# An inverse square root moved from GpSimd to VectorE in the layer norms that run inside four attention layers

## The chip, the cores and the metric

The kernel is one program on one core of a Trainium2 chip. The metric is the device time of that program in microseconds (us), from its first to its last instruction and what lies around them. The engines are named as the profile names them: PE is TensorE (matrix products, transposes), PEld its weight loads, DVE is VectorE, ACT is ScalarE, POOL is GpSimd, SP the engine that issues most DMAs.

## The reference, cut to what matters

Sixteen sequences of 112 tokens with 256 features go through four layers. Each layer is a cross attention against a context of 375 rows, then a feed-forward part, both on the normalised residual stream:

```python
def _layernorm(x, axis=-1, eps=1e-05):
    m = jnp.mean(x, axis=axis, keepdims=True)
    v = jnp.var(x, axis=axis, keepdims=True)
    return (x - m) / jnp.sqrt(v + eps)
...
x = x + _L0_xattn_ref(_layernorm(x), ctx_1024, ...)     # 16 heads of 16
x = x + _L0_ffn_ref(_layernorm(x), ...)                 # 8 experts, 1 chosen, one shared
x = x + _L1_xattn_ref(_layernorm(x), ctx_1024, ...)     # 1 head of 256
x = x + _L1_ffn_ref(_layernorm(x), ...)                 # 8 experts, 2 chosen, two shared
x = x + _L2_xattn_ref(_layernorm(x), ctx_1024, ...)     # 16 heads of 64
x = x + _L2_ffn_ref(_layernorm(x), ...)                 # 8 experts, 2 chosen
x = x + _L3_xattn_ref(_layernorm(x), ctx_1024, ...)     # 16 heads of 16
x = x + _L3_ffn_ref(_layernorm(x), ...)                 # expert 0 alone, then its own layer norm
```

The change touches the four norms ahead of the feed-forward parts: they are computed inside the attention, as soon as a pair of sequences has its new residual. Everything is 32-bit floating point.

## The kernel before

The kernel works layer after layer (L0 to L3), and each layer in three stages with a meeting of PE, DVE and ACT between them: a norm and transposes ahead of the attention, the attention, the feed-forward part. The attention goes over 16 sequences (called b) and in L0, L2 and L3 over 16 heads of each; one head is a **slot** here, numbered 0 to 15 within its sequence. L1 has one head, so one slot is a whole sequence.

The order of work in the attention is one list of steps, `Att.plan`, which PE, DVE and ACT each walk from front to back, doing their own share of each step. In every slot stand the scores of one head (PE line 895 or 900 or 903, the maximum on DVE line 1149, 1160 or 1153), the exponential of a head (ACT line 1196), the transposes of its probabilities (PE 914, copied by DVE 1169 or ACT 1203) and, in L0 and L3, every fourth slot the product with the values for four heads (PE 945). Between them the steps of `extras` are laid: the projections of the next sequence (`gen q`, `gen k`, `gen v`: PE 813, 833, 837; DVE 1060 or 1063, 1072), the split of q and k for an exact product (DVE 1033, 1035), and the steps that finish a sequence: `norm` (DVE 1130, 1133), `gen i` (PE 843), `gen o` (PE 857, DVE 1080 or 1077) and `stats` (DVE 1095).

After the `stats` of every odd sequence come the steps of the norm of that pair of sequences, `("ln", pair, i)` for i from 0 to `LN_STEPS`. With `LN_STEPS` of 4 these are: two `bn_aggr` (line 1107), variance plus epsilon into `newton` (1109), `nmr` = minus mean times `rstd` (1112), and `xn`, two instructions (1120). `rstd`, the inverse square root, is made by POOL between the third and the fourth (line 1299, power of minus one half). Then `gen n` has PE transpose `xn` (864), ACT copies it out (1239), and in L0 to L2 `gen r` multiplies by the router's weights (PE 871, DVE 1087 or 1089). POOL also stores `xn` to memory (1306) in L0 to L2, and in L3 adds a bias (1324).

`follow` places these steps: each one slot after the one before, `gen r` two slots after `gen n`. In L1 all steps of a pair's norm stand in one slot, and in every layer the steps of the last pair stand behind the last slot, where no other work is left. Every step of a norm waits on the semaphore `ln_dve` for the step before it.

Of the kernel before, what the change touches and what calls it, by code (L numbers as in the profile page):

```python
# [26 lines left out]
I32 = mybir.dt.int32  # L27
U8 = mybir.dt.uint8
U32 = mybir.dt.uint32
ALU = mybir.AluOpType  # L30
# [4 lines left out]
B = 16  # L35
S = 112
# [7 lines left out]
CHUNK = 4  # L44
NCH = B // CHUNK
TOK = CHUNK * S
EPS = 1e-5
# [59 lines left out]
LN_STEPS = 4  # L107
# [341 lines left out]
def build(nc, A):  # L449
    ctx = ExitStack()  # L450
    with ctx:
        sb = lambda name, shape, dt=F32: ctx.enter_context(nc.sbuf_tensor(name, shape, dt))
        sem = lambda name: ctx.enter_context(nc.semaphore(name))
# [24 lines left out]
        root = sb("root", [S, CHUNK])  # L478
# [53 lines left out]
        newton = sb("newton", [S, 2])  # L532
# [51 lines left out]
        ln = Ln(sem)  # L584
        fin = sem("final_chain")
        b2_added = sem("b2_added")
        rooted = sem("roots_by_pool")
# [369 lines left out]
        def att_vector(dve, t):  # L957
# [139 lines left out]
            def row_norm(pair, i):  # L1097

                at = ln.at(2 * L + 1)
                two = slice(2 * pair, 2 * pair + 2)  # L1100
                u, y = newton[:, :], rstd[:, two]
                before = [("stats", 2 * pair), ("stats", 2 * pair + 1)] + \
                     [("ln", pair, j) for j in range(1, LN_STEPS)]
                dve.wait_ge(ln.dve, at + t.row_steps[before[i]])
                if i < 2:
                    b = 2 * pair + i
                    ins = dve.bn_aggr(mv[:, b, :], stats[:, b, :])
                elif i == 2:
                    ins = dve.tensor_scalar(u, mv[:, two, 1], EPS, None, ALU.add)  # L1109
                elif i == 3:  # L1110
                    dve.wait_ge(rooted, L * (B // 2) + pair + 1)
                    ins = dve.scalar_tensor_tensor(out=nmr[:, two], in0=mv[:, two, 0], scalar=-1.0, in1=y,
                                                   op0=ALU.mult, op1=ALU.mult)
                else:
                    if t.moe and pair >= 2:
                        f = ffn[L]
                        dve.wait_ge(f.x_stored[pair % 2], f.x_stored0 + 16 * (pair // 2))
                        dve.wait_ge(t.gen_ready, t.g0 + t.gen_index("n", 2 * pair - 3) + 1)
                    for b in (2 * pair, 2 * pair + 1):
                        ins = dve.tensor_scalar(xnr(t, b), xb(b), rstd[:, b:b + 1], nmr[:, b:b + 1], ALU.mult, ALU.add)  # L1120
                    ins.then_inc(ln.xn, 1)
                    return
                ins.then_inc(ln.dve, 1)
# [170 lines left out]
        def reciprocal_root(pool, t, pair):  # L1294

            at = ln.at(2 * t.L + 1)
            two = slice(2 * pair, 2 * pair + 2)
            pool.wait_ge(ln.dve, at + t.row_steps[("ln", pair, 2)])
            pool.tensor_tensor(rstd[:, two], newton[:, :], root[:, 0:2], ALU.pow).then_inc(rooted, 1)  # L1299

        def store_tokens(pool, t, f):

            for pair in range(B // 2):
                reciprocal_root(pool, t, pair)
                pool.wait_ge(ln.xn, (2 * t.L + 1) * (B // 2) + pair + 1)
                pool.dma_start(xnd[f.L][pair * 2 * S:(pair + 1) * 2 * S, :].rearrange("(b s) d -> s b d", s=S),
                               xn[:, pair % 2, :, :]).then_inc(f.x_stored[pair % 2], 16)
# [9 lines left out]
        def add_b2(pool, t, f):  # L1317

            pool.wait_ge(f.w_landed, 16)
            for pair in range(B // 2):  # L1320
                reciprocal_root(pool, t, pair)
# [701 lines left out]
        def _(pool):  # L2023
# [8 lines left out]
            nc.gpsimd.memset(root[:, :], -0.5).then_inc(consts, 1)  # L2032
# [3 lines left out]
            pool.wait_ge(consts, 10)  # L2036
# [12 lines left out]
            pool.wait_ge(consts, 18)  # L2049
# [14 lines left out]
        def _(pe):  # L2064
            pe.wait_ge(consts, 19)
# [9 lines left out]
        def _(act):  # L2075
            act.wait_ge(consts, 19)
# [10 lines left out]
        def _(dve):  # L2087
            dve.wait_ge(consts, 19)
            dve.tensor_reduce(sel2[:, :], sel16[:, :].rearrange("p (j e) -> p e j", e=2), AX_X, ALU.add)\
                .then_inc(consts, 1)  # L2090
            dve.wait_ge(consts, 20)
# [112 lines left out]
```

## Time and profile before

| | us |
|---|---|
| median of 3 runs | 2652.26 (2651.37 to 2652.56) |
| the profiled execution | 2652.56, of it the span from first to last instruction 2650.8 |
| PE busy | 2301.7 (87% of the span) |
| DVE busy | 1263.3 (48%) |
| ACT busy | 1050.3 (40%) |
| POOL busy | 253.3 (10%) |

Busy shares are averages over the whole program. The attention of L0 lies at about 30 to 410 us, that of L1 at 800 to 890, of L2 at 1200 to 1902, of L3 at 2150 to 2500; what a change is worth has to be read in those stretches. Times in the rows further below are microseconds from the start of the span, and a row of the timeline names start, duration, engine, line, operation, output and inputs, and in square brackets how long the engine sat idle before and on what it waited.

### The profile page before, as it was taken

To read this page: it belongs to the slowest core of one execution; us is meant where nothing else is said; L and a number is where in the kernel's file an instruction comes from. 1 tells how busy PE (TensorE), PEld (TensorE's weight loads), DVE (VectorE), ACT (ScalarE), POOL (GpSimd) and SP (SyncE) were. 2 spreads that over 40 slices of the span, in tenths; PEclk is the share of its full clock that TensorE was granted. 3 is DMA by queue.
4 is the path that set the end of the run, shared out by engine and by line. 5 is a ranking of instruction groups with operands and counts; after the bars stand their busy time and mean duration, and the time that the engine had idled before them with its cause. 6 is when DMAs were issued, how large, how long until landed. Compare 5 with 4: busy or idle time off the path is not lost.

```text
span 2650.8 us, 45875 instructions
## 1 busy us (share of the span) xinstructions
PE 2301.7 (87%) x15952; PEld 1782.7 (67%) x15952; DVE 1263.3 (48%) x3635; ACT 1050.3 (40%) x2819; POOL 253.3 (10%) x288
## 2 busy tenths in 40 slices
PE   4889886999969599859999999999689579989893
PEld 3777774777757467547777778777467457777662
DVE  5777773222234522264444444444622457777405
ACT  2777771222113122124444444444212157777510
POOL 0000000111101044100000000000034200000000
PEclk8999996999969699969999999999889879999996
DMA  6877765222244212310000000000322378777200
GB/s 189 194 190 193 190 146 225 80 80 96 62 137 161 109 56 64 80 50 7 16 7 17 11 16 7 11 16 1 122 92 64 87 201 192 191 187 189 69 0 28
DMA packets 149806, 254.19 MB, mean 96 GB/s; under 512 B 14784, under 2 KB 124688, under 8 KB 146912
## 3 DMA queue, kind: packets, MB, share of 16 engines
q1 hardware_dynamic: 138640, 221.09, 30.8%
q0 software_dynamic: 10944, 30.16, 3.6%
q8 instruction: 136, 2.23, 0.4%
q14 instruction: 86, 0.70, 0.1%
HBM read 192.22 MB, written 58.98 MB: 95 GB/s over the span
## 4 chain that ended last, share of the span: by engine, by line
PE 72%; DVE 14%; issue 6%; ACT 4%; DMA 2%; PEld 1%; SPq 0%; POOL 0%; DVEq 0%; PEldq 0%; ACTq 0%; POOLq 0%
PE bank L1619 8%; PE bank L945 6%; PE bank L914 6%; PE bank L1649 6%; PE bank L822 5%; PE bank L826 5%; PE bank L1674 5%; PE bank L900 4%; PE bank L857 4%; PE bank L1662 3%; PE bank L813 3%; DVE arena L1149 3%; PE bank L837 2%; PE bank L1922 2%; PE bank L1908 2%
## 5 line engine op out<-in xcount | busy, mean ns | idle before, releaser
L914 PE MATMUL bank<-ident,arena 112*125 112x112 f32 x2352 | 369.7, 275 | 1.4 <-ACT arena L1203 1.2
L914 PEld LDWEIGHTS bank<-ident,arena 112*125 112x125 f32 x2352 | 340.5, 188 | 39.9 <-issue 2.6
L1196 ACT ACTIVATE arena<-arena,mx 112x375 f32<-112x375 f32 x512 | 309.3, 605 | 140.2 <-DVE mx L1149 136.1
L1149 DVE CUSTOM_DVE_ANT_0 arena<-bank,maskf 112x375 f32<-112x375 f32 x512 | 274.2, 542 | 91.9 <-PE bank L895 75.0
L895 PE MATMUL bank<-kS,qS 128*112 128x376 f32 x512 | 237.6, 465 | 31.5 <-DMA kS<-key_halves 21.2
L945 PE MATMUL bank<-arena 125*32 125x112 f32 (+1 forms) x4608 | 202.0, 264 | 57.7 <-DVE arena L1169 28.9
L1160 DVE TENSOR_REDUCE mx<-bank 112x1 f32<-112x375 f32 x256 | 129.0, 544 | 245.8 <-PE bank L900 245.3
L945 PEld LDWEIGHTS bank<-arena 125*32 125x32 f32 (+1 forms) x4608 | 147.4, 118 | 145.4 <-issue 67.9
L1619 PE MATMUL bank<-arena 128*128 x552 | 238.6, 555 | 3.4 <-ACT arena L1721 3.2
L1169 DVE COPY arena<-bank 125x336 f32<-125x336 f32 x448 | 214.5, 503 | 33.4 <-PE bank L914 33.4
L1196 ACT ACTIVATE arena<-bank,mx 112x375 f32<-112x375 f32 x272 | 156.0, 575 | 172.6 <-DVE mx L1160 150.0
L1203 ACT ACTIVATE arena<-bank 125x336 f32<-125x336 f32 x336 | 147.8, 441 | 72.6 <-PE bank L914 71.8
L1649 PE MATMUL bank<-arena 128*128 (+1 forms) x696 | 173.0, 380 | 0.0
L1299 POOL TENSOR_TENSOR rstd<-newton,root 112x2 f32<-112x2 f32 x32 | 22.6, 707 | 1538.3 <-DVE newton L1109 1538.3
L822 PE MATMUL bank<-ctx_halves,weight_halves 128*128 128x376 f32 x768 | 145.8, 342 | 7.3 <-DVE arena L1066 7.3
L1619 PEld LDWEIGHTS bank<-arena 128*128 128x128 f32 x552 | 103.5, 191 | 68.1 <-issue 48.8
L826 PE MATMUL bank<-weight_halves,ctx_halves 128*126 128x512 f32 x576 | 148.5, 403 | 0.0
L1674 PE MATMUL bank<-xnT,arena 128*128 128x224 f32 (+1 forms) x640 | 143.4, 369 | 3.4 <-DVE gather_id L1446 3.4
L1751 ACT ACTIVATE oT<-bank 128x224 f32<-128x224 f32 x80 | 28.5, 356 | 279.0 <-PE bank L1674 273.5
L822 PEld LDWEIGHTS bank<-ctx_halves,weight_halves 128*128 128x128 f32 x768 | 132.4, 191 | 7.5 <-DVE arena L1066 7.5
L1542 POOL DMA_INDIRECT results<-arena,scatter_id x94 | 93.2, 992 | 411.7 <-ACT arena L1743 332.4
L1674 PEld LDWEIGHTS bank<-xnT,arena 128*128 128x128 f32 (+1 forms) x640 | 111.1, 180 | 30.8 <-issue 16.2
(233 smaller groups left out, 3564.8 us busy)
## 6 DMA issues: line engine op xcount, KB each, us to landing
kS<-key_halves SPq DMA_DIRECT2D x256, 188.0 KB, 5.4
qS<-query_halves SPq DMA_DIRECT2D x128, 224.0 KB, 4.6
arena<-in_ctxT SPq DMA_DIRECT2D x64, 376.0 KB, 4.7
key_halves<-arena SPq DMA_DIRECT2D x64, 376.0 KB, 4.9
arena<-in_f_out SPq DMA_DIRECT2D x22, 768.0 KB, 4.4
query_halves<-arena SPq DMA_DIRECT2D x32, 448.0 KB, 3.8
arena<-in_f_up SPq DMA_DIRECT2D x4, 2816.0 KB, 19.3
arena<-results SPq DMA_DIRECT2D x20, 448.0 KB, 8.0
```

The source lines that it names most:

```text
L822: m = pe.matmul(dst[:, 0:SKE], wH[:, 0, wh, c * t.W + o * P:c * t.W + (o + 1) * P], ctxH[:, ch, c, :], **flags)
L826: m = pe.matmul(dst[0:KT + 1, 0:t.VW], ctxH[:, ch, c, o * KT:(o + 1) * KT + 1], wH[:, 1, wh, c * t.W + h * t.VW:c * t.W + (h + 1) * t.VW], ...
L895: m = pe.matmul(bank[g % 2][0:S, 0:SKE], qS[:, b % 2, h * S:(h + 1) * S].bitcast(F32R), kS[:, b % 2, h // 2 * SKE:(h // 2 + 1) * SKE].bitc ...
L914: m = pe.transpose(bank[2 + g % 2][0:KT, k * S:(k + 1) * S], pr[:, g % t.NR, k * KT:(k + 1) * KT], ident[0:S, 0:S])
L945: m = pe.matmul(out, v, pTv(t, g + j)[:, k, :], **flags)
L1149: dve.tensor_tensor_reduce(sm[:, g % 2, :], bank[g % 2][0:S, 0:SK], maskf[:, :], 1.0, 3e38, ALU.add, ALU.min, mx[:, g % t.NR:g % t.NR + 1])\
L1169: dve.tensor_copy(pTb(t, g), bank[2 + g % 2][0:KT, 0:NKT * S]).then_inc(t.pt_sbuf[1], 1)
L1196: act.activation(pr[:, g % t.NR, :], src, ACT.Exp, bias=mx[:, g % t.NR:g % t.NR + 1], scale=-1.0, accum_out=row_sum(t, b)[:, h:h + 1]).the ...
L1203: act.activation(pTb(t, g), bank[2 + g % 2][0:KT, 0:NKT * S], ACT.Copy).then_inc(t.pt_sbuf[0], 1)
L1619: ins = pe.matmul(bank[m % 2][:, 0:w * f.NU], xTb(n)[:, k, :], up[:, bass.ds(expert[n], 1), at:at + w * f.NU].rearrange("p e n -> p (e n)" ...
L1649: ins = pe.matmul(bank[4 + n % 2][:, 0:D], midT_of(f, m)[:, j * P:(j + 1) * P], w2, start=(q + j == 0), stop=(q == G - 1 and j == J - 1))
L1674: ins = pe.matmul(bank[6][0:w, u * 2 * S:(u + 1) * 2 * S], up[u][:, k, o:o + w], xnT[:, k, c * 2 * S:(c + 1) * 2 * S], start=(u + k == 0), ...
```

## The change

POOL no longer makes the inverse square root. `reciprocal_root`, its semaphore and the constant tile `root` are gone. DVE computes it in the steps of the norm instead: `LN_STEPS` goes from 4 to 15. Step 3 makes minus half of the variance plus epsilon, step 4 a first value from the number's bits taken as an integer, steps 5 to 13 are three rounds of Newton's method with three instructions each, step 14 makes `nmr` and step 15 `xn`. All of them are instructions on 112 partitions and 2 elements, but for the last. The counts of the semaphore `constants_ready` are lowered by the one constant that is gone.

```diff
-LN_STEPS = 4
+LN_STEPS = 15
...
-        newton = sb("newton", [S, 2])
+        newton = sb("newton", [S, 2, 4])
...
-                u, y = newton[:, :], rstd[:, two]
+                var, u, y, a = mv[:, two, 1], newton[:, :, 0], rstd[:, two], newton[:, :, 2]
+                half = newton[:, :, 1]
...
                 elif i == 2:
-                    ins = dve.tensor_scalar(u, mv[:, two, 1], EPS, None, ALU.add)
+                    ins = dve.tensor_scalar(u, var, EPS, None, ALU.add)
                 elif i == 3:
-                    dve.wait_ge(rooted, L * (B // 2) + pair + 1)
+                    ins = dve.tensor_scalar(half, u, -0.5, None, ALU.mult)
+                elif i == 4:
+                    ins = dve.tensor_scalar(y.bitcast(I32), u.bitcast(I32), -0.5, float(0x5f3759df), ALU.mult, ALU.add)
+                elif i < 14 and i % 3 == 2:
+                    ins = dve.tensor_tensor(a, y, y, ALU.mult)
+                elif i < 14 and i % 3 == 0:
+                    ins = dve.tensor_tensor(a, a, half, ALU.mult)
+                elif i < 14:
+                    ins = dve.scalar_tensor_tensor(out=y, in0=a, scalar=1.5, in1=y, op0=ALU.add, op1=ALU.mult)
+                elif i == 14:
                     ins = dve.scalar_tensor_tensor(out=nmr[:, two], in0=mv[:, two, 0], scalar=-1.0, in1=y,
                                                    op0=ALU.mult, op1=ALU.mult)
...
-        def reciprocal_root(pool, t, pair):
-
-            at = ln.at(2 * t.L + 1)
-            two = slice(2 * pair, 2 * pair + 2)
-            pool.wait_ge(ln.dve, at + t.row_steps[("ln", pair, 2)])
-            pool.tensor_tensor(rstd[:, two], newton[:, :], root[:, 0:2], ALU.pow).then_inc(rooted, 1)
-
         def store_tokens(pool, t, f):
 
             for pair in range(B // 2):
-                reciprocal_root(pool, t, pair)
```

The longer norm moves instructions in three places. The line numbers of the changed kernel differ by a few from those before (864 becomes 862, 1120 becomes 1128).

On DVE in L1, the norm of one pair, before: `mv` holds mean and variance, `lowest` is the first work for the next sequence's scores.

```order
L1095 BN_STATS stats<-x 112x6
L1107 BN_AGGR mv<-stats 112x2 x2
L1109 TENSOR_SCALAR newton<-mv 112x2
L1112 SCALAR_TENSOR_TENSOR nmr<-mv,rstd 112x2
L1120 TENSOR_SCALAR xn<-x,rstd,nmr 112x256 x2
L1153 TENSOR_REDUCE lowest<-bank 112x1
```

And in the changed kernel, from the first value of the root on:

```order
L1112 TENSOR_SCALAR rstd<-newton 112x2
L1114 TENSOR_TENSOR newton<-rstd 112x2
L1116 TENSOR_TENSOR newton<-newton 112x2
L1118 SCALAR_TENSOR_TENSOR rstd<-newton,rstd 112x2
L1114 TENSOR_TENSOR newton<-rstd 112x2
L1116 TENSOR_TENSOR newton<-newton 112x2
L1118 SCALAR_TENSOR_TENSOR rstd<-newton,rstd 112x2
L1114 TENSOR_TENSOR newton<-rstd 112x2
L1116 TENSOR_TENSOR newton<-newton 112x2
L1118 SCALAR_TENSOR_TENSOR rstd<-newton,rstd 112x2
L1120 SCALAR_TENSOR_TENSOR nmr<-mv,rstd 112x2
L1128 TENSOR_SCALAR xn<-x,rstd,nmr 112x256 x2
```

Eleven instructions more stand in a row, each behind the one before it, ahead of `xn` and of the next `lowest`. The same rows stand in a row behind the last slot of L0, L2 and L3.

On DVE in L0, slots 8 to 10 of sequence 3, in which the norm of the first pair (sequences 0 and 1) ends in the changed kernel, before: 1149 (shown as ISA) is a head's maximum, 1169 the copy of transposed probabilities.

```order
L1080 TENSOR_TENSOR x<-bank,x 112x256
L1149 ISA arena,mx<-bank,maskf 112x375
L1149 ISA mx 112x1
L1095 BN_STATS stats<-x 112x6
L1072 TENSOR_TENSOR arena<-bank,bvB 125x8x2x16
L1149 ISA arena,mx<-bank,maskf 112x375
L1149 ISA mx 112x1
L1169 COPY arena<-bank 125x336
```

And in the changed kernel:

```order
L1120 SCALAR_TENSOR_TENSOR nmr<-mv,rstd 112x2
L1078 TENSOR_TENSOR x<-bank,x 112x256
L1157 ISA arena,mx<-bank,maskf 112x375
L1157 ISA mx 112x1
L1128 TENSOR_SCALAR xn<-x,rstd,nmr 112x256 x2
L1093 BN_STATS stats<-x 112x6
L1070 TENSOR_TENSOR arena<-bank,bvB 125x8x2x16
L1157 ISA arena,mx<-bank,maskf 112x375
L1157 ISA mx 112x1
L1177 COPY arena<-bank 125x336
```

`xn` has moved here from slot 14 of the sequence before, and one small instruction of the norm stands in each slot between.

On PE in L0, from slot 15 of sequence 2 to slot 1 of sequence 3, before: 864 transposes `xn`, 871 is the router's product, 813 and 833 are the projections of q and k.

```order
L945 MATMUL bank<-arena 32x112 x12
L864 MATMUL bank<-ident,xn 128x112 x4
L895 MATMUL bank<-kS,qS 112x376
L914 MATMUL bank<-ident,arena 125x112 x3
L813 MATMUL bank<-xnT,arena 128x112 x4
L895 MATMUL bank<-kS,qS 112x376
L914 MATMUL bank<-ident,arena 125x112 x3
L871 MATMUL bank<-wR,xnT 112x8 x4
L833 MATMUL bank<-arena 128x375 x2
```

In the changed kernel they stand in slots 10 and 12 of sequence 3, among the projections of v (835):

```order
L835 MATMUL bank<-arena 125x256 x2
L893 MATMUL bank<-kS,qS 112x376
L912 MATMUL bank<-ident,arena 125x112 x3
L862 MATMUL bank<-ident,xn 128x112 x4
L893 MATMUL bank<-kS,qS 112x376
L912 MATMUL bank<-ident,arena 125x112 x3
L943 MATMUL bank<-arena 32x112 x12
L835 MATMUL bank<-arena 125x256 x2
L893 MATMUL bank<-kS,qS 112x376
L912 MATMUL bank<-ident,arena 125x112 x3
L869 MATMUL bank<-wR,xnT 112x8 x4
```

The transposes now stand between a head's transposes and the next product with the values (943), no longer right behind such a product. The same shift of 11 slots holds in L2 and L3.

## Rows read from the trace of the kernel before

**Rows 1.** The page's chain that ended last, shares by engine.

```profile
PE 72%; DVE 14%; issue 6%; ACT 4%; DMA 2%; PEld 1%; SPq 0%; POOL 0%; DVEq 0%; PEldq 0%; ACTq 0%; POOLq 0%
```

**Rows 2.** The page's groups: the root on POOL (busy, mean ns, idle before).

```profile
L1299 POOL TENSOR_TENSOR rstd<-newton,root 112x2 f32<-112x2 f32 x32 | 22.6, 707 | 1538.3 <-DVE newton L1109 1538.3
```

**Rows 3.** Timeline of L1, the norm of one pair: start, duration, instruction.

```profile
850.62 0.17 DVE L1109 TENSOR_SCALAR newton<-mv 112x2 f32<-112x2 f32 x1
...
850.88 0.70 POOL L1299 TENSOR_TENSOR rstd<-newton,root 112x2 f32<-112x2 f32 x1 [6.66 <-DVE newton L1109]
...
851.69 0.16 DVE L1112 SCALAR_TENSOR_TENSOR nmr<-mv,rstd 112x2 f32<-112x2 f32 x1 [0.91 <-POOL rstd L1299]
851.89 0.74 DVE L1120 TENSOR_SCALAR xn<-x,rstd,nmr 112x256 f32<-112x256 f32 x2
...
852.77 0.57 PE L864 MATMUL bank<-ident,xn 112*128 112x112 f32 x4 [0.47 <-DVE xn L1120]
```

**Rows 4.** Waits, 820 to 892 us: total us, times, longest.

```profile
PE bank L864 <- DVE xn L1120: 9.6, 8, 3.4
```

**Rows 5.** Timeline of PE, transposes of the last pair of L0, L2 and L3.

```profile
406.28 0.98 PE L864 MATMUL bank<-ident,xn 112*128 112x112 f32 x4 [3.33 <-DVE xn L1120]
...
1900.09 0.57 PE L864 MATMUL bank<-ident,xn 112*128 112x112 f32 x4 [3.33 <-DVE xn L1120]
...
2498.31 0.98 PE L864 MATMUL bank<-ident,arena 112*128 112x112 f32 x4 [3.31 <-DVE arena L1120]
```

**Rows 6.** Timeline of L0's routing: small DVE instructions that depend on each other.

```profile
420.43 0.17 DVE L1419 TENSOR_SCALAR blk<-pos 112x16 f32<-112x16 f32 x1
420.64 0.17 DVE L1420 TENSOR_SCALAR blk<-blk 112x16 f32<-112x16 f32 x1
```

**Rows 7.** Timeline of L0: a small DVE instruction ahead of independent work.

```profile
199.32 0.16 DVE L1109 TENSOR_SCALAR newton<-mv 112x2 f32<-112x2 f32 x1
199.39 0.54 DVE L1149 CUSTOM_DVE_ANT_0 arena<-bank,maskf 112x375 f32<-112x375 f32 x1
```

**Rows 8.** Timeline of PE in L0, from slot 10 of sequence 6 and of 7.

```profile
194.31 0.52 PE L895 MATMUL bank<-kS,qS 128*112 128x376 f32 x1
...
196.16 0.78 PE L945 MATMUL bank<-arena 125*32 125x112 f32 x24 [0.52 <-DVE arena L1169]
...
201.16 0.78 PE L945 MATMUL bank<-arena 125*32 125x112 f32 x24 [0.31 <-ACT arena L1203]
...
216.93 0.53 PE L895 MATMUL bank<-kS,qS 128*112 128x376 f32 x1
...
223.68 0.58 PE L945 MATMUL bank<-arena 125*32 125x112 f32 x14 [0.24 <-ACT arena L1203]
```

**Rows 9.** Timeline of DVE in L0: the same step of three sequences.

```profile
207.52 0.24 DVE L1130 RECIPROCAL rinv<-sums 112x16 f32<-112x16 f32 x1
...
229.11 0.24 DVE L1130 RECIPROCAL rinv<-sums 112x16 f32<-112x16 f32 x1
...
251.72 0.24 DVE L1130 RECIPROCAL rinv<-sums 112x16 f32<-112x16 f32 x1
```

**Rows 10.** Timeline of DVE in L0, the end of slot 10.

```profile
195.51 0.50 DVE L1169 COPY arena<-bank 125x336 f32<-125x336 f32 x1
```

**Rows 11.** Busy us in stretches; the column after POOL is PE's granted clock.

```profile
875.00:880.00 5.00, 2.93 (x23) 2.64 (x23) 2.51 (x11) 0.42 (x2) 0.84 (x2) 1.00 0.00 0
880.00:885.00 5.00, 4.08 (x19) 2.78 (x17) 2.00 (x7) 0.54 (x1) 0.55 (x1) 0.65 0.16 46
1345.00:1391.00 46.00, 46.00 (x354) 36.02 (x351) 21.46 (x45) 20.30 (x52) 0.00 (x0) 1.00 0.03 9
```

**Rows 12.** Timeline of PE, end of L1: router product, transposes of the last two pairs.

```profile
874.50 0.86 PE L871 MATMUL bank<-wR,xnT 128*112 128x8 f32 x8
...
879.71 0.57 PE L864 MATMUL bank<-ident,xn 112*128 112x112 f32 x4 [2.07 <-DVE xn L1120]
...
887.48 0.98 PE L864 MATMUL bank<-ident,xn 112*128 112x112 f32 x4 [3.39 <-DVE xn L1120]
```

More of the change, by code:

```diff
@@ L477, in build @@
         epsc = sb("epsc", [P, 1])
-        root = sb("root", [S, CHUNK])
         def part(at, n, rows=P):
@@ L586, in build @@
         b2_added = sem("b2_added")
-        rooted = sem("roots_by_pool")
         padded = sem("values_padded")
@@ L1320, in add_b2 @@
             for pair in range(B // 2):
-                reciprocal_root(pool, t, pair)
                 pool.wait_ge(t.gen_ready, t.g0 + t.gen_index("n", 2 * pair + 1) + 1)
@@ L2031, in _ @@
             nc.gpsimd.memset(ones[:, :], 1.0).then_inc(consts, 1)
-            nc.gpsimd.memset(root[:, :], -0.5).then_inc(consts, 1)
             nc.gpsimd.memset(tri[:, :], 1.0).then_inc(consts, 1)
@@ L2035, in _ @@
                 .then_inc(consts, 1)
-            pool.wait_ge(consts, 10)
+            pool.wait_ge(consts, 9)
             nc.gpsimd.tensor_copy(lane[:, :], lanei[:, :]).then_inc(consts, 1)
@@ L2048, in _ @@
                                     base=0, pattern=[[-16, 8]], channel_multiplier=1).then_inc(consts, 1)
-            pool.wait_ge(consts, 18)
+            pool.wait_ge(consts, 17)
             nc.gpsimd.affine_select(out=sel16[:, :], in_=sel16[:, :], compare_op=ALU.is_ge, fill=0.0,
@@ L2064, in _ @@
         def _(pe):
-            pe.wait_ge(consts, 19)
+            pe.wait_ge(consts, 18)
             for L in range(4):
@@ L2075, in _ @@
         def _(act):
-            act.wait_ge(consts, 19)
+            act.wait_ge(consts, 18)
             for L in range(4):
@@ L2087, in _ @@
         def _(dve):
-            dve.wait_ge(consts, 19)
+            dve.wait_ge(consts, 18)
             dve.tensor_reduce(sel2[:, :], sel16[:, :].rearrange("p (j e) -> p e j", e=2), AX_X, ALU.add)\
                 .then_inc(consts, 1)
-            dve.wait_ge(consts, 20)
+            dve.wait_ge(consts, 19)
             dve.wait_ge(loaded["x"], 16)
```

## The prediction, written before the changed kernel was timed

> **What bounds the kernel now.** I read the page first. The chain that ended last is PE for 72% and DVE for 14% [rows 1]: what DVE gains or loses counts only where a PE step waits for it. The root on POOL takes 0.707 us, 32 times [rows 2]; POOL's idle time before it means nothing. So I looked at the places where a norm runs, and there are two kinds.
>
> The first is serial. In L1 the timeline shows the third step of the norm at 850.62, the root on POOL, `nmr` at 851.69, `xn` at 851.89, and PE idle for 0.47 us until `xn` is there [rows 3]. The table of waits counts eight such waits of PE in L1's attention, one for each pair, 9.6 us in all [rows 4]; the last pair's is 3.39 us [rows 12]. Behind the last slot of L0, L2 and L3 PE idles 3.3 us for the same `xn` [rows 5]. These are 8 + 3 = 11 places where the norm is the path.
>
> The second is the inside of L0, L2 and L3, seven pairs in each, 21 in all, with one step of a norm in each slot. There the question is what a small DVE instruction costs, and what it costs to have `xn`, PE's transposes and the router's product 11 slots later.
>
> **The change, the serial places.** From the start of the third step to the start of `nmr` it takes 851.69 - 850.62 = 1.07 us now [rows 3]. Afterwards twelve intervals lie between the same two starts (eleven new instructions behind the third step). One interval is that of small dependent DVE instructions: 420.64 - 420.43 = 0.21 us, and `nmr` to `xn` is 851.89 - 851.69 = 0.20 us [rows 3, 6]. I take 0.205: 12 x 0.205 = 2.46 us, 1.39 us more than now. All of it moves PE, since PE already waits at each of the eleven: 11 x 1.39 = **15.3 us**. In L1 what stands behind the norm on DVE is the minimum of the next scores, and so ACT's exponential, and PE's transposes of it; they shift by the same 1.39 us as PE's own work, so they are not charged again. With 0.20 or 0.21 the sum is 14.6 or 15.9.
>
> A row shows that a dependent small instruction starts 0.04 us after the former's 0.17 us have ended [rows 6]. The Trainium skill, "VectorE: DVE Perf Modes", section "The DRAIN you can't avoid", says that a semaphore between chained instructions costs nothing extra and that their number is what counts. By it an interval would be the duration alone, which is the fourth rival below.
>
> **The change, inside the loops.** A small instruction ahead of independent work delays that work by 199.39 - 199.32 = 0.07 us, not by its 0.16 [rows 7]. What such a delay costs the loop can be read, because in L0 the even sequences have the five steps of a norm in slots 10 to 14 and the odd ones have none, with the same other work: from slot 10's scores to the product with the values behind slot 15 it is 201.16 - 194.31 = 6.85 us with them and 223.68 - 216.93 = 6.75 us without [rows 8]. So four small instructions, `xn` and the wait for POOL cost 0.10 us together: DVE has room there, and taking POOL's part out of these slots gives next to nothing. Eleven further steps fall into slots 15 to 9, where I count about four in which DVE stands between PE's steps (the copy, `rinv`, the splits): 4 x 0.08 = 0.32 us. For L0 and L3, 14 pairs, **4.5 us**.
>
> `xn` moves to slot 9, ahead of the evacuation of the values and so of the copy at 195.51 for which PE idles 0.52 us before the product [rows 8, 10]. Its two instructions hold DVE for about 0.65 us, some 0.2 of which fit in DVE's gap: PE's product comes 0.45 us later. Against it PE's transposes leave slot 15, where their time was paid in full, and now stand inside that wait. The period with norm, transposes and router's product is 251.72 - 229.11 = 22.61 us, that without 229.11 - 207.52 = 21.59 [rows 9]; split like their busy times of 0.57 and 0.86 us [rows 3, 12], an estimate, 0.41 of the 1.02 us are the transposes' and 0.61 the router's product's. The first is traded for `xn`, the second stays a PE cost in slot 12. So I count **0** for the moves. Bounds on a pair's sum: below, 0.41 saved and nothing paid; above, eleven times 0.16 and 0.45, which is 2.2 us.
>
> In L2 PE is busy for 46.00 of 46.00 us while DVE is busy for 21.46 [rows 11]: the small steps are covered, and PE's moved steps are the same work. **0**, with some tenths of a microsecond either way in each pair from who waits for a bank. The cover would be gone only where a step stood behind a wait for PE and ahead of PE's next input, and with 24 us of DVE idle in 46 I see none.
>
> POOL loses 32 instructions and one fill of a constant. Its queue then holds only the stores of `xn`, which wait for `xn` as before and are 1.39 us later at the end of a stage; they stay ahead of the first gather, which waits for the routing.
>
> **The clock.** The transposes at the end of L2 still ran at the high level (0.57 us), those of L0 and L3 and of L1's last pair after such a wait at the low one (0.98 us) [rows 5, 12]; the levels are 2.4 and 1.2 GHz. With a wait of 4.7 instead of 3.3 us I count the low level at the end of L2 too: 0.4 us for the transposes and about as long as they again for the router's product. **1.0 us**.
>
> **Sum.** 15.3 + 4.5 + 0 + 1.0 = 20.8 us on the profiled execution's 2652.56 us (span 2650.8 and 1.8 around it), 0.3 us above the median of the runs: 2652.26 + 20.8 = **2673 us**, 0.8% slower. No change in a measurement of this kernel is 0.2%, that is 5.3 us.
>
> **The rivals.**
> 1. *DVE becomes the bound in the loops of L0 and L3.* For it: a DVE step with a wait of its own may hold the queue for its full 0.16 us, and `xn` lands in the slot whose copy PE waits for. Against: the 0.10 us of slots 10 to 15 [rows 8]. At the upper bound, 14 x 2.2 = 31 instead of 4.5: 2699 us.
> 2. *The clock falls earlier in L1.* For it: PE's granted clock is 1.00 until 880 us and then falls, in a stretch in which PE waited 2.07 us before a pair's transposes [rows 11, 12]; these waits become 1.4 us longer each, and those of the earlier pairs too. Against: the earlier pairs wait only 0.47 us, 1.9 afterwards. If the fall comes one pair sooner, the PE work between 871.6 and 881.5 us, about 7.9 us busy at the high level, takes twice as long: 2681 us. The Trainium skill, "TensorE: Matmul & The Clock Gate", section "HAM oscillation — how this bites in real kernels", tells of such a fall after idle gaps of PE that come back with every tile. No row here shows the full clock lost in an early pair of L1.
> 3. *The later transposes and router's products are hidden, and the kernel is not slower.* The new place puts PE's transposes ahead of a product that waits 0.52 us [rows 8], where before they stood behind one. The price, if all of it vanished: 0.57 for the transposes and 0.86 for the router's product [rows 3, 12], the first 21 times and the second 14 times, 24 us, against 20.8: 2649 us. It decides from 15.5 us hidden on, with 5.3 to spare. Against: in L2 PE has no idle time into which 10 of these 24 us could go [rows 11], and in L0 and L3 the wait that would take them is lengthened by `xn`.
> 4. *A chained instruction costs only its duration, and the loops are free.* 12 x 0.16 - 1.07 = 0.85 us, eleven times, is 9.4 us, and 2 us for the rest: 2664 us. Against: the interval of 0.21 us, which this trace shows for instructions of the same size [rows 6].
>
> **Chances.** The forecast 0.62, rival 1 0.12, rival 2 0.12, rival 3 0.04, rival 4 0.10. The forecast's own range is 2668 to 2680 (14.6 to 15.9 for the chains, nothing to 11 us for the loops). The range that should hold 8 in 10 takes in rival 4's and rival 2's times: 2663 to 2686. Rival 3 lies within 0.2% with 0.02 to 0.03 of its chance, and the rest, if the chains are cheaper too, is faster by over 0.2%: 0.02. Within 0.2%: 0.04, with the low end of rival 4. Slower: 0.94.
>
> **What would show it.** In the changed kernel: in L1 the third step to `nmr` takes 2.4 to 2.5 us, PE's longest waits for `xn` are about 1.9 us in the early pairs and 4.7 in the last, and the total of these waits is 9.6 + 11 us. At the ends of L0, L2 and L3 PE waits 4.7 us for `xn`. The period of two sequences in L0, now 44.2 us, is 44.5, and DVE's busy time grows by 352 small instructions, 0.16 us each, some 55 us, of which hardly any shows in L2. If the periods of L0 and L3 grow by over 1 us, rival 1 is right; if the clock is low in L1 before the transposes of pair 6, rival 2; if the chain takes 1.9 us, rival 4. The forecast is wrong as a whole if PE doesn't wait longer for `xn` in L1.

## The result, and the profile after

| | before | after |
|---|---|---|
| median of the runs, us | 2652.36 | 2667.86 (2663.22 to 2672.43) |
| ratio, 95% interval | | 1.0056 [1.0041, 1.0072] |
| the profiled execution, us | 2652.56 | 2676.24, span 2674.5 |
| DVE busy, us | 1263.3 | 1298.7 |
| POOL busy, us | 253.3 | 229.0 |

The changed kernel is slower by 15.5 us. The forecast was 20.8 us, and its range held the time. The profiled execution is the longest of all eight of the changed kernel (2662.98 to 2676.24 us), so below a single step is read from it, and a sum only with that in mind. One execution of the experiment e14 ran at a mean granted clock of 0.618 and took 4046.81 us; it is in that run's median, not in its ratio.

The parts of the profile's page that answer to rows 1, of the changed kernel, busy time first and then the chain of waits by engine:

```profile
PE 2309.0 (86%) x15952; PEld 1789.2 (67%) x15952; DVE 1298.7 (49%) x3987; ACT 1051.3 (39%) x2819; POOL 229.0 (9%) x255
...
PE 72%; DVE 15%; issue 6%; ACT 3%; DMA 2%; PEld 1%; SPq 0%; DVEq 0%; PEldq 0%; ACTq 0%; POOLq 0%
```

DVE has gained one per cent of the chain. DVE's busy time has grown by 35 us where 352 instructions of 0.16 us were announced as some 55: where they follow or precede other work they overlap it, as the rows at 207.41 and 207.48 below show.

**The serial places.** The timeline of DVE and PE in L1, one pair, changed kernel (rows 3 show the same stretch before):

```profile
848.70 0.30 DVE L1106 BATCH_NORM_AGGREGATE mv<-stats 112x2 f32<-112x6 f32 x2
849.03 0.17 DVE L1108 TENSOR_SCALAR newton<-mv 112x2 f32<-112x2 f32 x1
849.23 0.17 DVE L1110 TENSOR_SCALAR newton<-newton 112x2 f32<-112x2 f32 x1
849.44 0.17 DVE L1112 TENSOR_SCALAR rstd<-newton 112x2 int32<-112x2 int32 x1
849.64 0.16 DVE L1114 TENSOR_TENSOR newton<-rstd 112x2 f32<-112x2 f32 x1
...
851.22 0.16 DVE L1118 SCALAR_TENSOR_TENSOR rstd<-newton,rstd 112x2 f32<-112x2 f32 x1
851.41 0.16 DVE L1120 SCALAR_TENSOR_TENSOR nmr<-mv,rstd 112x2 f32<-112x2 f32 x1
851.61 0.74 DVE L1128 TENSOR_SCALAR xn<-x,rstd,nmr 112x256 f32<-112x256 f32 x2
...
852.49 0.57 PE L862 MATMUL bank<-ident,xn 112*128 112x112 f32 x4 [1.78 <-DVE xn L1128]
```

From the third step (849.03) to `nmr` (851.41) it is 2.38 us: twelve intervals of 0.198 us. Before it was 1.07 [rows 3], so a norm on the path costs 1.31 us more, and PE's wait grows from 0.47 to 1.78 us, by just this. The table of waits for 820 to 912 us, which answers to rows 4, has

```profile
PE bank L862 <- DVE xn L1128: 20.0, 8, 4.7
```

20.0 instead of 9.6 us in all, eight times, the longest 4.7. And at the ends of L0, L2 and L3, PE's first transposes behind the last norm [rows 5]:

```profile
409.76 0.98 PE L862 MATMUL bank<-ident,xn 112*128 112x112 f32 x4 [4.64 <-DVE xn L1128]
...
1918.35 0.98 PE L862 MATMUL bank<-ident,xn 112*128 112x112 f32 x4 [4.63 <-DVE xn L1128]
...
2521.61 0.98 PE L862 MATMUL bank<-ident,arena 112*128 112x112 f32 x4 [4.63 <-DVE arena L1128]
```

4.64 us of waiting for 3.3, and the transposes of L2 have gone from 0.57 to 0.98 us, as forecast.

**The loops.** The period of two sequences is read from one `stats` to the one two sequences later, as the mean of four pairs in the middle of a stage. The experiments are set beside it, since the verdicts rest on this table; the last column is L1's attention from its first `stats` to its last.

| us | L0 | L2 | L3 | L1, first to last |
|---|---|---|---|---|
| before | 44.20 | 90.37 | 43.24 | 72.9 |
| after | 44.65 | 89.83 | 43.40 | 89.4 |
| e1, POOL's root, later steps | 44.39 | 89.82 | 43.13 | 73.1 |
| e3, Newton inside the loops only | 44.66 | 89.82 | 43.41 | 74.9 |
| e10, small instructions doubled | 44.98 | 89.83 | 43.69 | 85.2 |
| e5b, seven extra matmuls in L1 | 44.65 | 89.82 | 43.44 | 80.4 |
| e6, two rounds | 44.69 | 90.28 | 43.51 | 80.9 |
| e13, L1's norm in two slots | 44.66 | 89.83 | 43.41 | 69.0 |
| e12, POOL's root, both moves | 44.20 | 89.82 | 43.12 | 64.6 |
| e14, router's product later in L2 | 44.21 | 90.08 | 43.24 | 73.0 |

L0 has become 0.45 us a pair longer, L3 0.16 longer, and L2, for which nothing was forecast, 0.54 **shorter**. In rows, L0 and then L2 of the changed kernel, the reciprocals of two sequences that are a pair apart:

```profile
207.41 0.15 DVE L1114 TENSOR_TENSOR newton<-rstd 112x2 f32<-112x2 f32 x1
207.48 0.25 DVE L1138 RECIPROCAL rinv<-sums 112x16 f32<-112x16 f32 x1
...
252.13 0.24 DVE L1138 RECIPROCAL rinv<-sums 112x16 f32<-112x16 f32 x1
...
1432.67 0.24 DVE L1138 RECIPROCAL rinv<-sums 112x16 f32<-112x16 f32 x1
...
1522.47 0.24 DVE L1138 RECIPROCAL rinv<-sums 112x16 f32<-112x16 f32 x1
```

252.13 - 207.48 = 44.65, against 44.20 before [rows 9], and 1522.47 - 1432.67 = 89.80. In L2 before the same two rows are

```profile
1414.12 0.24 DVE L1130 RECIPROCAL rinv<-sums 112x16 f32<-112x16 f32 x1
...
1504.47 0.24 DVE L1130 RECIPROCAL rinv<-sums 112x16 f32<-112x16 f32 x1
```

90.35 us. The two rows of L0 at 207.41 and 207.48 also show what a small instruction costs what follows it: 0.07 us, as in rows 7.

**What L2 gained.** PE's timeline in L2 before, at one router's product (line 871), which stands between two projections to q (813), and below it PE in the changed kernel at the same two projections:

```profile
1408.80 1.84 PE L813 MATMUL bank<-xnT,arena 128*128 128x112 f32 x15
1410.47 0.86 PE L871 MATMUL bank<-wR,xnT 128*112 128x8 f32 x8
1411.51 2.04 PE L813 MATMUL bank<-xnT,arena 128*128 128x112 f32 x16 [0.17 <-DVE arena L1066]
```

```profile
1428.35 3.74 PE L811 MATMUL bank<-xnT,arena 128*128 128x112 f32 x32
```

The product takes 0.86 us, and then PE waits 0.17 us more. The kernel has two result banks for these steps; the product takes the one that the second projection would have had, so that one needs the first projection's bank back from DVE (line 1066). The two projections with the product between them hold PE 1.12 us longer than the two in one piece (from the first one's start to PE's next step 4.79 against 3.67 us). In the changed kernel the 32 matmuls run in one piece and the product stands elsewhere, where it moves PE's next step by 0.79 us; the transposes move it by 0.38 instead of 0.59 us. Together this is the 0.54 us of the period. By the rows it is a gain of the steps' new places, not of the new root; e1 tests it.

This also shows what the prediction's window row left out. The 46 us of [rows 11] are half of L2's period, the half without the router's product. Over a whole period, before, it is (length of the window, then PE's busy time)

```profile
1300.00:1390.37 90.37, 90.18 (x693) 70.41 (x692) 41.21 (x90) 38.47 (x98) 1.48 (x2) 1.00 0.04 12
```

0.19 us of idle time in all, so at least 0.35 of the 0.54 us were PE's busy time at a bad place, which no idle time shows.

**The clock.** Windows of 10 us in L1, before and then changed (busy time and count of PE, PEld, DVE, ACT, POOL, then PE's granted clock, DMA share and GB/s); rows 11 have the later stretches before:

```profile
824.00:834.00 10.00, 9.52 (x66) 7.97 (x65) 5.47 (x18) 3.46 (x10) 1.42 (x2) 1.00 0.57 187
874.00:884.00 10.00, 7.93 (x50) 6.42 (x49) 3.66 (x15) 1.26 (x3) 1.40 (x2) 0.87 0.08 25
```

```profile
824.00:834.00 10.00, 8.22 (x44) 6.26 (x43) 4.65 (x19) 2.82 (x8) 0.74 (x1) 0.83 0.51 171
834.00:844.00 10.00, 8.22 (x50) 6.38 (x49) 6.45 (x26) 3.27 (x9) 0.69 (x1) 1.00 0.51 170
...
874.00:884.00 10.00, 9.26 (x54) 7.38 (x54) 4.65 (x19) 3.63 (x10) 0.66 (x1) 0.83 0.08 23
884.00:894.00 10.00, 7.70 (x39) 7.15 (x40) 3.33 (x16) 1.35 (x3) 0.66 (x1) 0.66 0.09 25
```

In this execution the granted clock fell to 1.2 GHz for a short stretch as early as 827 us, again at 875 and 885, and for good at 899. Before it fell once, at 881.5. PE had waited 1.78 us for `xn` once a pair, and the falls at 827 and 875 came within 1 us of the ends of two such waits (826.17 and 873.91). Of the 16.5 us that L1's attention grew in this execution 9.2 are seven waits of 1.31 us; the other 7.3 I put down to the clock.

Such a wait does not always bring a fall, and a fall does not need the new root. The experiment e10 has the same code in L1 and the same five waits of 1.78 us, but its clock stayed at 1.00 up to 880.5 us, behind a longer wait of 3.04 us; its L1 took 85.2 us, 3.1 more than the waits explain. In e3, which has POOL's root in L1 as before, the clock was low for 3.4 us from 874.2, and L1 took 2.0 us more than before. Two windows of e10, and below them one of e3:

```profile
824.00:834.00 10.00, 8.22 (x55) 6.75 (x54) 6.29 (x26) 3.05 (x9) 0.04 (x2) 1.00 0.54 179
874.00:884.00 10.00, 6.96 (x41) 6.29 (x41) 5.22 (x24) 1.80 (x4) 0.66 (x1) 0.83 0.08 25
```

```profile
874.00:884.00 10.00, 7.94 (x50) 7.29 (x48) 3.42 (x13) 1.76 (x5) 1.39 (x2) 0.83 0.09 25
```

So the clock's share of L1 differs from execution to execution, between 2.0 and 7.3 us in these three.

### The profile page after: what moved, and what is told of

It reads as the page before. It is cut to its first block, busy times and chain, and to the rows that moved or that the text cites. A ratio compares the mean times of both kernels' runs of the same rounds, so it can differ in the third digit from the quotient of the medians.

```text
span 2674.5 us, 46156 instructions
## 1 busy us (share of the span) xinstructions
PE 2309.0 (86%) x15952; PEld 1789.2 (67%) x15952; DVE 1298.7 (49%) x3987; ACT 1051.3 (39%) x2819; POOL 229.0 (9%) x255
## 4 chain that ended last, share of the span: by engine, by line
PE 72%; DVE 15%; issue 6%; ACT 3%; DMA 2%; PEld 1%; SPq 0%; DVEq 0%; PEldq 0%; ACTq 0%; POOLq 0%
PE bank L1618 8%; PE bank L943 6%; PE bank L912 6%; PE bank L1648 6%; PE bank L824 5%; PE bank L820 5%; PE bank L1673 5%; PE bank L898 4%; PE bank L855 4%; PE bank L811 3%; PE bank L1661 3%; DVE arena L1157 3%; PE bank L1921 2%; PE bank L835 2%; PE bank L1907 2%
## 5 line engine op out<-in xcount | busy, mean ns | idle before, releaser
L1211 ACT ACTIVATE arena<-bank 125x336 f32<-125x336 f32 x336 | 148.3, 442 | 86.2 <-PE bank L912 85.2
L1618 PEld LDWEIGHTS bank<-arena 128*128 128x128 f32 x552 | 103.9, 192 | 68.4 <-issue 49.0
L893 PEld LDWEIGHTS bank<-kS,qS 128*112 128x112 f32 x512 | 90.9, 178 | 62.5 <-DMA kS<-key_halves 22.1
L1648 PEld LDWEIGHTS bank<-arena 128*128 128x128 f32 x696 | 121.6, 190 | 11.2 <-issue 0.3
```

What stands on the lines that cost most here:

```text
L893: m = pe.matmul(bank[g % 2][0:S, 0:SKE], qS[:, b % 2, h * S:(h + 1) * S].bitcast(F32R), kS[:, b % 2, h // 2 * SKE:(h // 2 + 1) * SKE].bitc ...
L1211: act.activation(pTb(t, g), bank[2 + g % 2][0:KT, 0:NKT * S], ACT.Copy).then_inc(t.pt_sbuf[0], 1)
L1618: ins = pe.matmul(bank[m % 2][:, 0:w * f.NU], xTb(n)[:, k, :], up[:, bass.ds(expert[n], 1), at:at + w * f.NU].rearrange("p e n -> p (e n)" ...
L1648: ins = pe.matmul(bank[4 + n % 2][:, 0:D], midT_of(f, m)[:, j * P:(j + 1) * P], w2, start=(q + j == 0), stop=(q == G - 1 and j == J - 1))
```

## The experiments

My theory after the result: a chain of twelve intervals where PE waits for it, a small cost of the small instructions in L0 and L3, a gain of L2 from the steps' new places, and a clock that falls sometimes. Its rivals: the loops carry the loss (DVE), or the clock does.

**e1: the old root, the steps as late as in the changed kernel.** On the kernel before, in `follow`:

```diff
-                at += 2 if step[1] == "r" else 1
+                at += 2 if step[1] == "r" else 12 if step[0] == "ln" and step[2] == 4 else 1
```

> The root stays on POOL; only the last step of the norm (xn), PE's transposes and the router's product come 11 slots later in L0, L2 and L3. Theory (the parts add up: places and small steps cost apart): the moves alone give in two sequences of L2 about 89.85 us where before has 90.37, in L0 44.35 (before 44.20, changed kernel 44.65), in L3 43.10 (43.24, 43.40), no change in L1 and at the stage ends; total about 2649 us, 3 to 4 below before. Rival (what L2 gained came from POOL's instruction being gone, and what L0 lost from the places): L2 stays at 90.37, L0 is at 44.65, total 2654.

Measured: 2648.92 us (2643.91 to 2651.50) against 2652.90, ratio 0.9983 [0.9974, 0.9993]. The periods are 44.39, 89.82 and 43.13: the new places alone give the whole gain of L2 (-0.55 a pair), cost 0.19 in L0 and save 0.11 in L3. Seven pairs each make -3.3 us, and -4.0 were measured. `xn` and the transposes at their new place are no loss (L3, which has no router's product). L0 comes out 0.30 us a pair dearer than L3, and the router's product is the step that L0 has and L3 has not; that it carries the 0.30 is inferred, since no run moved it alone in L0.

**e3: Newton's steps inside the loops only.** On the changed kernel; L1 and the last pair of each layer take POOL's root again.

```diff
+def ln_steps(L, pair):
+
+    return 4 if L == 1 or pair == B // 2 - 1 else LN_STEPS
...
+            if ln_steps(t.L, pair) < LN_STEPS:
+                two = slice(2 * pair, 2 * pair + 2)
+                pool.wait_ge(ln.dve, ln.at(2 * t.L + 1) + t.row_steps[("ln", pair, 2)])
+                pool.tensor_tensor(rstd[:, two], newton[:, :, 0], root[:, 0:2], ALU.pow).then_inc(rooted, 1)
...
```

> The changed kernel with POOL's root put back in L1 and for the last pair of L0, L2 and L3, eleven places. Theory (the eleven serial chains are the loss): the loops keep the changed kernel's periods (44.65, 89.8, 43.4), the third step to nmr is 1.07 us again at the eleven places, total 2652 to 2653 us, as before. Rival (the loss sits elsewhere, in the clock or in the loops): the total stays above 2658.

Measured: 2654.14 us (2650.91 to 2655.43), ratio 1.0004 [0.9994, 1.0014], a little over what was expected. Without the eleven serial places the kernel is no slower than before, though 21 of 32 norms are Newton's. Against the changed kernel's ratio of 1.0056 some 14 us are the serial places', with what the clock did beside them. The rival that DVE is the bound in the loops falls. The small instructions themselves cost 44.66 - 44.39 = 0.27 us a pair in L0, 0.28 in L3 and nothing in L2 (e3 against e1).

**e10: each of the eleven new steps twice inside the loops.** On the changed kernel, behind each of them a like instruction of no use, which waits for the one before of its kind:

```diff
+                if H > 1 and pair < B // 2 - 1 and 2 < i < 14:
+                    doubles.append(i)
+                    dve.wait_ge(doubled, len(doubles) - 1)
+                    dve.tensor_scalar(newton[:, :, 3], mv[:, two, 1], EPS, None, ALU.add).then_inc(doubled, 1)
```

> The changed kernel with each of the eleven new small steps inside the loops of L0, L2 and L3 doubled (a second small instruction with a wait of its own, its result unused): 231 more DVE instructions. Theory (small steps cost 0.28 us per pair in L0 and L3, through DVE, and nothing in L2): L0 44.9 to 45.0 us, L3 43.7, L2 89.8, total 4 us above the changed kernel. Rival A (they are hidden, the 0.28 came from the later xn): periods stay. Rival B (each costs its full 0.16 us): L0 and L3 1.7 us longer each pair, L2 too, total 20 to 35 us more.

Measured: 2674.35 us (2667.56 to 2677.02), 1.0083 [1.0066, 1.0100]. The periods of L0, L2 and L3 grew by 0.33, 0.00 and 0.29 us (of L0's four middle pairs one was disturbed; the others grew by 0.29): eleven more small instructions cost again what the first eleven did, 0.03 us each, and nothing in L2. Both rivals fall. Seven pairs of both make 4.3 us; 6.0 us were measured between the two kernels' distances from before, within their intervals.

**e5 and e5b: PE kept at work while it waits for `xn` in L1.** On the changed kernel, ahead of that wait, matmuls of an identity whose result is written over; e5 has 14 of them, e5b 7.

```diff
+                    for _ in range(7 if H == 1 else 0):
+                        pe.matmul(dst[:, 0:P], ident[:, :], ident[:, :], start=True, stop=True)
                     pe.wait_ge(ln.xn, (2 * L + 1) * (B // 2) + b // 2 + 1)
```

> The changed kernel; in L1 PE multiplies a constant tile by itself 14 times into the bank that the transposes overwrite, while it waits for xn (about 1.5 of the 1.8 us). Theory (the extra loss of the profiled run in L1 is the clock falling after PE's longer waits): the granted clock stays 1.00 through L1 until its last pairs, L1's attention grows over before by 7 x 1.31 = 9.2 us to the last stats instead of 16.5, total 2662 to 2666 with less spread than the changed kernel's 2663 to 2676. Rival (the low stretches in L1 have nothing to do with PE's waits): they stay, and the time is that of the changed kernel or above it.

Measured: 2670.77 us (2664.60 to 2672.81), 1.0061 [1.0043, 1.0078], no better. The clock stayed at 1.00 up to 907 us, but 14 matmuls took 3.2 us, more than the wait of 1.8 that they were to fill, and from an odd sequence's `stats` to the next it took 7.31 instead of 6.14 us. The number was too high, so it was halved:

> As the run with 14 extra products, with 7: these were 0.225 us each, 3.2 us for 14, more than the wait of 1.8 us that they were to fill, so that run was longer by 1.17 us for each pair of L1. Theory (filling PE's wait keeps the clock and costs nothing): L1's odd-to-next period is the changed kernel's 6.14 us, the clock stays 1.00 until the last two pairs, total about 2662 to 2665 us. Rival (keeping PE busy does not pay at all): 2668 or more.

Measured: 2664.32 us (2664.26 to 2664.97), 1.0044 [1.0029, 1.0059]. PE's timeline in L1 and the windows of e5b:

```profile
847.90 1.74 PE L859 MATMUL bank<-ident 128*128 128x128 f32 x14
849.76 0.60 PE L864 MATMUL bank<-ident,xn 112*128 112x112 f32 x4
```

```profile
824.00:834.00 10.00, 9.88 (x69) 8.30 (x68) 6.23 (x26) 3.27 (x9) 0.74 (x1) 1.00 0.58 187
...
874.00:884.00 10.00, 8.62 (x72) 8.14 (x71) 5.71 (x26) 3.27 (x8) 0.66 (x1) 1.00 0.07 22
884.00:894.00 10.00, 8.30 (x66) 7.52 (x65) 5.52 (x27) 1.26 (x3) 0.66 (x1) 1.00 0.09 26
```

The seven (shown as 14 passes) end just as `xn` comes, the same distance is 6.08 us, and the clock is 1.00 up to 901 us, past L1's last `stats` at 894.9. Of the nine traces without the extra matmuls eight have the clock fall before L1's last `stats` (the ninth is e12, whose PE hardly waits there), in both with them it falls 6 to 7 us behind it. So keeping PE at work holds the clock here, and it takes away the fall in L1 that the kernel before had too. The four runs lie within 0.7 us of each other, those of the changed kernel over 9.2 us. That the clock in L1 made the difference isn't shown: e5, whose clock held in L1 as well, spreads over 8.2 us, and the kernel before over 5.4. Over the whole program the changed kernel's time does go with its mean granted clock (0.931 in its slowest execution, 0.939 in one of its fastest). What the uneven clock in L1 cost at the median is 3.5 us by these two kernels, but their intervals overlap; that it cost something in the profiled execution is shown (L1 80.4 against 89.4 us), its mean is not settled.

**e6: two rounds instead of three**, for nine instructions' delay instead of twelve; the inverse root is less exact by it.

```diff
-LN_STEPS = 15
+LN_STEPS = 12
...
-                elif i < 14 and i % 3 == 2:
+                elif i < 11 and i % 3 == 2:
...
```

> The changed kernel with two rounds of Newton's method instead of three (three small instructions fewer for each pair, the last step at 12). Theory (0.198 us for each chained instruction at eleven places): third step to nmr 2.38 - 0.59 = 1.79 us, total 6.5 us below the changed kernel, about 2661 us; loops within 0.1 us a pair. Rival (the chain is not the price): less than 2 us gained.

Measured: 2667.73 us (2666.65 to 2668.90), 1.0057 [1.0042, 1.0073]: a miss. The chain is 1.79 us as expected, 0.59 shorter. But with three steps fewer, `follow` puts the transposes three slots earlier, and there the gain of L2 is gone (90.28; by the period its transposes cost 0.84 us a pair instead of 0.38, and PE waits 0.19 us for ACT right behind them). 11 x 0.59 = 6.5 us saved, 7 x 0.45 + 7 x 0.04 + 7 x 0.11 = 4.2 us lost again; the 2.3 us that should be left did not show in the total (0.1), where the intervals of about 4 us would hide them. I had changed two things with one number, and priced one. By its total alone this run would speak for its rival; the chain and the waits in its trace (PE's early waits for `xn` in L1 are 1.19 instead of 1.78 us) speak against it.

**e13: the norm of L1 over two slots.** On the changed kernel, in the plan of L1: three steps in the slot as before, the rest one slot later, with other work of PE between.

```diff
-                    extras[at] += [("ln", b // 2, i) for i in range(LN_STEPS + 1)]
-                    extras[at + 1].append(gen("n", b))
-                    extras[at + 2].append(gen("r", b))
+                    extras[at] += [("ln", b // 2, i) for i in range(3)]
+                    extras[at + 1] += [("ln", b // 2, i) for i in range(3, LN_STEPS + 1)]
+                    extras[at + 2].append(gen("n", b))
+                    extras[at + 3].append(gen("r", b))
```

> The changed kernel with L1's norm spread over two slots: steps 0 to 2 as now, steps 3 to 15 a slot later, transposes and router's product another slot later. Theory (in L1 the chain costs only because PE is sent to wait for it in the very next step): PE does not wait for xn in L1's loop, its seven pairs lose the 1.31 us and the 0.47 us that before had, total 2655 to 2657 us. Rival (DVE itself is then what L1 waits for, since its chain of 2.4 us stands ahead of the next sequence's evacuation): L1's pair period stays above 10 us and the total above 2661.

Measured: 2652.27 us (2647.26 to 2656.81), 0.9996 [0.9987, 1.0006], better than expected. DVE's and PE's timelines of e13 in L1:

```profile
843.37 0.16 DVE L1111 TENSOR_SCALAR newton<-newton 112x2 f32<-112x2 f32 x1
...
845.55 0.16 DVE L1121 SCALAR_TENSOR_TENSOR nmr<-mv,rstd 112x2 f32<-112x2 f32 x1
845.75 0.73 DVE L1129 TENSOR_SCALAR xn<-x,rstd,nmr 112x256 f32<-112x256 f32 x2
...
846.95 0.55 PE L863 MATMUL bank<-ident,xn 112*128 112x112 f32 x4
```

The chain is as long as ever (eleven intervals of 0.198 us from 843.37 to `nmr`), but PE's transposes come later and without a wait; its waits for `xn` in L1's attention sum to 6.6 us in three places instead of 20.0 in eight. The same instructions on the same engine cost little where nothing waits for them. In the middle of L1 two sequences take 8.73 us here and 8.74 in e12, which has POOL's root: there the chain costs nothing. Of the 4.4 us by which L1 is longer here than in e12, 4.1 fall on the last four sequences, where there is less work of PE to lay between; the clock too fell before the last `stats` here (879.3 against 882.0 us) and after it in e12, and how the two share these 4.1 us was not separated.

**e12: the version that the runs point to.** The kernel before with POOL's root, L1's norm in two slots as in e13, and the later steps of e1 in L2 and L3 alone:

```diff
-                at += 2 if step[1] == "r" else 1
+                at += 2 if step[1] == "r" else 12 if step[0] == "ln" and step[2] == 4 and self.L in (2, 3) else 1
...
```

> The root on POOL as before, with what the runs so far showed to pay: the last step, transposes and router's product 11 slots later in L2 and L3 (not in L0), and L1's norm over two slots. Theory (the parts add up): L2 -0.55 us and L3 -0.11 us for each of six to seven pairs, in L1 the waits of PE for xn of the first seven pairs (6.2 us) gone: 2652.9 - 3.9 - 0.7 - 6 = about 2642 us. Rival (L1's gain is given back because the next scores' minimum on DVE waits for POOL's root anyway): about 2648 us.

Measured: 2637.13 us (2636.00 to 2638.69), 0.9942 [0.9929, 0.9956], faster than the kernel before and the changed one, and 5 us faster than expected: L1 with its end gave 10.4 us instead of 6. Its timeline in L1, DVE, PE and POOL:

```profile
840.10 0.16 DVE L1113 SCALAR_TENSOR_TENSOR nmr<-mv,rstd 112x2 f32<-112x2 f32 x1
...
843.67 0.55 PE L865 MATMUL bank<-ident,xn 112*128 112x112 f32 x4
...
846.32 0.17 DVE L1110 TENSOR_SCALAR newton<-mv 112x2 f32<-112x2 f32 x1
846.40 0.55 DVE L1154 TENSOR_REDUCE lowest<-bank 112x1 f32<-112x375 f32 x1
...
846.58 0.70 POOL L1300 TENSOR_TENSOR rstd<-newton,root 112x2 f32<-112x2 f32 x1 [4.57 <-DVE newton L1110]
```

POOL's root runs beside DVE's next minimum (846.58 and 846.40): the other engine is not the cost, waiting for it was. L1's attention is 64.6 us long, 8.3 less than before; L2 and L3 give 7 x (0.55 + 0.12) = 4.7, and L1's last norm up to the feed-forward part 2.1 us.

**e14: which move helped L2.** On the kernel before, the router's product two slots later, in L2 alone:

```diff
-                at += 2 if step[1] == "r" else 1
+                at += (4 if self.halves else 2) if step[1] == "r" else 1
```

> The kernel before with one edit: in L2 the router's product stands two slots later, among the projections of k and no longer between the two projections of q of the next sequence; the transposes stay where they were. Theory (of L2's 0.55 us for a pair, 0.33 came from the router's product having stood between the two q projections, where PE waits for DVE's evacuation of the first, 0.17 us): two sequences of L2 take 90.04 us instead of 90.37, total about 2 us below before. Rival (the gain needs the transposes' new place, or stretches among the projections of v): L2 stays at 90.3 to 90.4, total as before.

Measured: 2652.90 us against 2651.89, ratio 1.0002 [0.9992, 1.0012], where about 2 us less were expected; the interval reaches from 2.1 us less to 3.2 us more, so the total can barely tell. The period of L2 is 90.08, 0.29 us shorter: this is the router's product leaving the two projections. The other 0.25 of the changed kernel's gain is left for the transposes' place (by the rows above 0.33 and 0.21). The 2.0 us of seven pairs are not seen in the total. In the profiled execution they were given back behind the loop: from L2's last `stats` to the feed-forward part's first it took 211.1 instead of 208.7 us. The windows there, before and then e14, cover the same 80 us:

```profile
1880.00:1960.00 80.00, 48.55 (x269) 36.51 (x269) 35.02 (x98) 9.06 (x23) 12.16 (x13) 0.72 0.39 151
```

```profile
1880.00:1960.00 80.00, 48.70 (x247) 36.64 (x248) 33.12 (x94) 8.05 (x20) 12.75 (x14) 0.68 0.39 152
```

The clock fell earlier against the end of the loop (1897.2 us, 3.2 after the last `stats`; before 1902.1, 4.8 after) and stayed low longer, 51.2 instead of 44.4 us. The stretch varies over the profiled executions of all kernels, from 208.7 to 212.9 us, of which the longer wait for the last `xn` explains 1.3 where the root is Newton's; what sets the rest was not found.

## Why the prediction was right, point by point

- **The serial places, 15.3 us.** Right. Eleven, at 1.31 instead of 1.39 us each, make 14.4 us; the interval was 0.198 instead of 0.205 us. e3 takes them out and the loss goes; e13 covers seven of them and the loss goes too. Rival 4 (9.4 us, a chain of 1.9) is refuted: the chain is 2.38 us. The Trainium skill, "VectorE: DVE Perf Modes", section "The DRAIN you can't avoid", says that the semaphore between chained instructions costs nothing extra. As the prediction read it, the chain would be twelve durations of 0.16, 1.92 us; the trace shows 0.04 us more at each dependent pair. Whether that is the semaphore's no run here shows, since none left it out.
- **Small steps in the loops, 4.5 us.** Right: 7 x (0.27 + 0.28) = 3.9 us. e10 confirms the price by doubling it. That four of the eleven steps carry it, at 0.08 us each, was a count that no run tests. Rival 1 (DVE the bound) is refuted.
- **The moved steps in L0 and L3, 0.** Nearly: 7 x (0.19 - 0.11) = 0.6 us, but out of two effects. The trade of transposes for `xn` saves 0.11 a pair in L3, and L0 is 0.30 dearer than that, most likely by the router's product, which I had counted as unchanged. That they nearly cancel is luck.
- **L2, 0 with tenths either way.** The step that failed. It is -0.54 us a pair, 3.8 us; the tenths were there, but all one way, and the sum had them at 0. I argued that PE is busy for 46.00 of 46.00 us [rows 11] and that its moved steps are the same work, so nothing that moves can help. That row covers the half of the period without the router's product, and so not the wait of 0.17 us for a bank. Nor can any busy time show that the product between two projections costs 1.12 us and elsewhere 0.79. A busy share of 100% says that an engine has no visible gap, not that the order of its work has no price. Rival 3's mechanism (moved steps cheaper) was at work there, with a sixth of its size.
- **The clock, 1.0 us at the end of L2.** There the transposes went from 0.57 to 0.98 us as said, but the stretch grew by 2.9 us beyond the chain in the profiled execution. In L1 I took the early waits of 1.9 us to be harmless. By the test set beforehand (the clock low ahead of the transposes of pair 6), rival 2 came true in that execution, beside the forecast and not in its place: the low clock cost L1 about 7 us there. But that sign was too weak: e3, without the chain in L1, shows it too and lost 2.0 us there, so not all of the 7 need be the change's. I had also missed that pair 5 already waited 1.73 us before (at 871.57), not 0.47. The Trainium skill, "TensorE: Matmul & The Clock Gate", section "HAM oscillation — how this bites in real kernels", tells of a clock that falls after idle gaps of PE which come back with every tile. The trace agrees in part: two falls came right behind recurring gaps of 1.78 us, and in the two kernels whose gaps were filled with matmuls none came before 901 us, but the same gaps brought no early fall in e10's execution.
- **The sum.** 14.4 + 3.9 + 0.6 - 3.8 = 15.1 us are explained without the clock, and 15.5 were measured at the median; in the profiled execution 23.7, of which about 9 are left for the clock. The nearness of 15.1 and 15.5 is partly luck: the traces have 2 to 7 us of the clock in L1, and e5b, with the clock held there, is 3.6 us below this sum, in part because it has no fall in L1 where the kernel before has one at 881.5. The forecast of 20.8 us was 5.3 too high: 3.8 for L2, 0.9 for the chain, 1.0 for the clock, which the 15.1 leave out, less 0.4 that stay unexplained. The serial places, three quarters of the forecast, were understood; they carry it.

## What to carry to other kernels

Before an operation goes to another engine, ask where its consumer waits: twelve small dependent DVE instructions cost 2.4 us where PE waits for the last of them and 0.3 us where they lie one by one between other work. A hand-over to POOL and back takes 1.07 us on the path and costs nothing beside it, so the cure for a serial norm was to let its halves stand one slot apart (L1 and its end 10.4 us shorter in e12), not a faster root. When a parameter also sets where later steps fall, measure the new places apart from the new work: here they had opposite signs. And when a window is to stand for a loop, let it span a whole period.

## What the runs showed of the hardware

- Small dependent DVE instructions (112 partitions x 2 elements) start every 0.198 us, 0.16 of it their duration; an independent one behind such an instruction starts 0.07 us after it, and in loops with room the whole cost was 0.03 us each.
- With a gap of 1.78 us in PE's work once a pair, the granted clock fell at 827 and 875 us in one execution and not before 880.5 in another (e10); with seven matmuls in 1.74 us in each gap it held up to 901 us.
- How long PE stays at the low clock behind L2's end differed by up to 10 us (44.4 to 54.6) between profiled executions of kernels whose work there is nearly the same, and in e14's took back a gain of 2 us ahead of it.
